# Queries in rows for the last cross attention of a two-layer decoder, and the order of the third part set anew

## The reference

```python
def _L1_xattn_ref(x, context, Wq, Wk, Wv, Wo, bo):   # context: 64 keys of width 96 per sequence
    h, d = (16, 64)
    q = (x @ Wq).reshape(b, n, h, d).transpose(0, 2, 1, 3)
    k = (context @ Wk).reshape(b, -1, h, d).transpose(0, 2, 1, 3)
    v = (context @ Wv).reshape(b, -1, h, d).transpose(0, 2, 1, 3)
    attn = softmax(einsum('bhid,bhjd->bhij', q, k) * d ** -0.5, axis=-1)
    out = einsum('bhij,bhjd->bhid', attn, v)
    return out.transpose(0, 2, 1, 3).reshape(b, n, h * d) @ Wo + bo
x = _layernorm(x + _L1_xattn_ref(x, ctx_768, ...), axis=-1)
```

## Time and profile before

| what | us |
|---|---|
| median of three runs (1770.81 to 1782.97) | 1771.91 |
| the profiled execution's own time | 1776.66 |
| its span, first to last instruction | 1774.6 |
| part one and experts, up to part three's first transposition | about 653 |
| part three, seven full rounds of 133.0 | 931 |
| its last round | 99.2 |

### The profile page before, as it was taken

The page is one execution under the profiler, slowest core; times in us unless marked ns, Lnnn a source line. Parts: engine busy times, 40 slices in busy tenths (PEclk is TensorE's granted clock), DMA queues, the critical chain, the costliest instruction groups (busy, mean ns, idle before and its releaser), DMA issues.

```text
span 1774.6 us, 41025 instructions
## 1 busy us (share of the span) xinstructions
PE 1612.1 (91%) x17280; PEld 1053.8 (59%) x17280; DVE 1086.2 (61%) x2249; ACT 815.9 (46%) x1516; POOL 237.4 (13%) x402
## 2 busy tenths in 40 slices
PE   4899999999978878999999999999999999999985
PEld 1655555555536754675675675675675675675663
DVE  5177777877755454386386387387377277277254
ACT  1456655565542224445345445445445445445423
POOL 1011101110114710011011011011011011011011
PEclk9899999999988879999999999999999999999998
DMA  8331111111118740011011011011011010000000
GB/s 265 151 124 58 53 51 65 53 58 52 54 46 171 117 153 24 20 43 37 16 46 37 7 54 37 2 60 37 1 61 37 2 61 30 8 25 28 5 1 7
DMA packets 64999, 95.68 MB, mean 54 GB/s; under 512 B 9425, under 2 KB 47298, under 8 KB 64083
## 3 DMA queue, kind: packets, MB, share of 16 engines
q1 hardware_dynamic: 61491, 89.20, 15.0%
q0 software_dynamic: 2560, 3.46, 2.2%
q10 hardware_dynamic: 768, 0.40, 0.1%
HBM read 56.03 MB, written 38.80 MB: 53 GB/s over the span
## 4 chain that ended last, share of the span: by engine, by line
PE 72%; DVE 15%; ACT 5%; issue 4%; POOL 2%; DMA 1%; ACTq 0%; DVEq 0%; POOLq 0%; PEldq 0%
PE psum L898 7%; PE psum L804 6%; PE psum L990 6%; PE psum L646 5%; PE psum L885 4%; PE psum L661 3%; PE psum L856 3%; PE psum L671 3%; PE psum L813 3%; ACT prob L1156 3%; DVE kt L1280 3%; DVE va L1280 3%; PE psum L939 2%; PE psum L799 2%; PE psum L703 2%
## 5 line engine op out<-in xcount | busy, mean ns | idle before, releaser
L1156 ACT ACTIVATE prob<-psum 128x1024 f32<-128x1024 f32 (+1 forms) x352 | 322.7, 945 | 329.8 <-PE psum L813 96.0
L1280 DVE TENSOR_REDUCE w_shared<-psum 128x4 bf16<-128x1024 f32 (+1 forms) x160 | 192.8, 1224 | 136.7 <-PE psum L710 94.7
L1458 POOL TENSOR_TENSOR rstd<-moments,eps 128x2 f32<-128x2 f32 x64 | 15.4, 241 | 1005.4 <-DVE moments L1201 1005.4
L1280 DVE TENSOR_REDUCE kt<-psum 128x4 bf16<-128x1024 f32 (+2 forms) x112 | 134.9, 1218 | 15.3 <-PE psum L735 11.5
L804 PE MATMUL psum<-qt,kt 64*128 64x256 f32 x1024 | 131.4, 376 | 0.0
L898 PE MATMUL psum<-prob,v_big 128*64 128x256 f32 x1024 | 124.6, 385 | 0.0
L804 PEld LDWEIGHTS psum<-qt,kt 64*128 64x128 f32 x1024 | 98.6, 189 | 9.9
L939 PE MATMUL psum<-prob,va 128*32 128x256 f32 (+1 forms) x1536 | 95.4, 369 | 1.2 <-ACT prob L1156 1.1
L898 PEld LDWEIGHTS psum<-prob,v_big 128*64 128x64 f32 x1024 | 67.8, 136 | 43.1 <-issue 11.9
L1308 DVE TENSOR_TENSOR qt<-qt,psum 128x1024 f32<-128x1024 f32 x32 | 39.0, 1221 | 85.5 <-PE psum L966 85.0
L1280 DVE TENSOR_REDUCE va<-psum 128x4 bf16<-128x1024 f32 x64 | 76.0, 1215 | 7.3 <-PE psum L747 7.3
(11 more groups left out here) (330 smaller groups left out, 3269.1 us busy)
## 6 DMA issues: line engine op xcount, KB each, us to landing
zd<-kx SPq DMA_DIRECT2D x24, 512.0 KB, 6.0
union<-zd SPq DMA_DIRECT2D x16, 768.0 KB, 4.3
w_late<-ad SPq DMA_DIRECT2D x16, 512.0 KB, 3.7
w_late<-vd SPq DMA_DIRECT2D x16, 512.0 KB, 4.6
ad<-union SPq DMA_DIRECT2D x16, 256.0 KB, 2.1
vd<-union SPq DMA_DIRECT2D x16, 256.0 KB, 2.0
xg<-union SPq DMA_DIRECT2D x16, 192.0 KB, 1.9
w_late<-in_w1T SPq DMA_DIRECT2D x1, 2816.0 KB, 9.8
```

The source lines that it names most:

```text
L1156: nc.scalar.activation(prob_of[a][s][:, slot + 2 * i:slot + 2 * i + 2, 0:n], v.pair(step, i)[:, :, 0:n], ACT.Exp, scale=a.scale).then_inc( ...
L1280: nc.vector.tensor_reduce(dst, src, axis=AX.X, op=ALU.max).then_inc(v.free(step), 1)
```

## The change

L1X alone is computed in another way, and part three's order is new.

- CK, N, P, D and B of L1X are gone, as are the bf16 copies, `ones_x` and `shift_big`.
- S of L1X is one step per half of the queries (128): fp32 matmuls of `xt_x` with all of `a_x`, 16 heads times 64 keys in two banks. DVE takes each row's maximum per head and writes scores minus maximum to SBUF (`by_query`, in `prob`'s slots 4 to 7).
- A new step E per half: ACT takes the exponential in SBUF; DVE sums, takes the reciprocal of 16 columns and multiplies.
- T of L1X is eight transpositions of the weights per half, which ACT copies to `by_key` (`prob`'s slots 0 to 3).
- W of L1X goes by halves of the queries instead of halves of the heads; the matmuls are as many and as large as before.
- D and B remain for L1 only; counters of semaphores follow; three semaphores are merged into others.
- `TURNS3` and `AHEAD3` are new: 144 steps a round instead of 154.

```diff
+def context_scores_steps(s):
+    st = lambda kind, *n: [(kind, L1X, s, i) for i in n]
+    return st("XT", 0) + st("S", 0, 1) + st("E", 0, 1) + st("T", 0, 1) + st("W", 0, 1) + st("L", 0)
...
     main = lambda s: (project_steps(L1, s) + head_steps(L1, s)
-                      + tail_steps(L1, s, [("CK", L1X, s, 0)])
-                      + [("XT", L1X, s, 0)] + project_steps(L1X, s) + head_steps(L1X, s) + tail_steps(L1X, s)
+                      + tail_steps(L1, s) + context_scores_steps(s)
                       + [("XT", L1F, s, 0)] + project_steps(L1F, s) + head_steps(L1F, s) + tail_steps(L1F, s))
...
-AHEAD1, AHEAD3 = (22, 17, 6, 0, 0, 0, 0), (16, 23, 15, 15, 4, 4)
+AHEAD1, AHEAD3 = (22, 17, 6, 0, 0, 0, 0), (16, 22, 15, 15, 4, 4)
... # tensor_step
                 elif a is L1X:
-                    for t in range(2):
-                        last = mm(banks[:, t, :], xb[s][:, 128 * t:128 * t + 128], a_xb[s][:, 512 * which:512 * which + 512],
-                                  start=True, stop=True)
+                    for half in range(2):
+                        last = mm(banks[:, half, :], xt_x[s][:, 128 * which:128 * which + 128],
+                                  a_x[s][:, 512 * half:512 * half + 512], start=True, stop=True)
...
-                    chunks = [(4 * g + 2 * gg + x, banks[:, gg, 256 * x:256 * x + 256], x) for gg in range(2) for x in range(2)]
-                    for c, cols, x in chunks:
-                        both = flat(sel_h[:, 2 * c:2 * c + 2, :])[:, CTX:CTX + 128]
-                        mm(cols, both, shift_big[s], start=(x == 0), stop=False, skip_group_check=True)
-                    for c, cols, x in chunks:
-                        last = mm(cols, a_x[s][:, 128 * c:128 * c + 128], xt_x[s], start=False, stop=True,
-                                  skip_group_check=True)
+                    weights = flat(prob[s][:, 4 + 2 * g:6 + 2 * g, :])
+                    for u in range(8):
+                        last = nc.tensor.transpose(banks[:, u // 4, 128 * (u % 4):128 * (u % 4) + 128],
+                                                   weights[:, 128 * u:128 * u + 128], ident[:, :])
...
+                elif a is L1X:
+                    t = step[3]
+                    for u in range(8):
+                        last = mm(bank[:, t * 128:(t + 1) * 128], by_key[s][t][:, 128 * u:128 * u + 128], vw_x[s][:, u, :],
+                                  start=(u == 0 and t == 0), stop=(u == 7), skip_group_check=True)
... # scalar_step
+            elif kind == "E":
+                act.wait_ge(*v.drained(("S", a, s, step[3])))
+                weights = by_query[s][step[3]]
+                nc.scalar.activation(weights, weights, ACT.Exp, scale=a.scale).then_inc(y.exp_done[s], 1)
+            elif kind == "T" and a is L1X:
+                act.wait_ge(*v.filled(step))
+                copy(by_key[s][step[3]], flat(v.pair(step))).then_inc(v.free(step), 1)
... # vector_step
+            elif kind == "S" and a is L1X:
+                t, scores = step[3], flat(v.pair(step)).rearrange("p (h k) -> p h k", h=16)
+                dve.wait_ge(*v.filled(step))
+                nc.vector.tensor_reduce(largest[s][t], scores, axis=AX.X, op=ALU.max).then_inc(y.r_split[s], 1)
+                dve.wait_ge(y.r_split[s], v.at(9, 4 + t))
+                tt(by_query[s][t], scores, largest[s][t].unsqueeze(2).to_broadcast([128, 16, CTX]), ALU.subtract).then_inc(
+                    v.free(step), 1)
+            elif kind == "E":
+                t = step[3]
+                dve.wait_ge(y.exp_done[s], v.at(2, 1 + t))
+                nc.vector.tensor_reduce(total[s][t], by_query[s][t], axis=AX.X, op=ALU.add).then_inc(y.r_split[s], 1)
+                dve.wait_ge(y.r_split[s], v.at(9, 6 + 2 * t))
+                nc.vector.reciprocal(total[s][t], total[s][t]).then_inc(y.r_split[s], 1)
+                dve.wait_ge(y.r_split[s], v.at(9, 7 + 2 * t))
+                tt(by_query[s][t], by_query[s][t], total[s][t].unsqueeze(2).to_broadcast([128, 16, CTX]), ALU.mult).then_inc(
+                    y.r_parts[s], 1)
```

More of the change, by code:

```diff
@@ L165, in fills @@
     if kind == "P":
-        sums = ["D"] if a.big and step[3] == 0 else []
         if a is L1:
-            return sums + ["O"]
-        if a is L1X:
-            return sums
+            return ["D", "O"] if step[3] == 0 else ["O"]
         return ["O"] if step[3] == 0 else []
@@ L563, in q_cast @@
             def q_cast(self, a, s):
-                cast = lambda x: ("XT" if x is L1X else "C", x, s, 0)
-                return self.count([cast(x) for x in LAYERS[self.tag]], cast(a))
+                return self.count([("C", x, s, 0) for x in LAYERS[self.tag] if x is not L1X], ("C", a, s, 0))
             def k_cast(self, a):
-                return self.at(1, 1) if self.tag == "p1" else self.at(3, CASTS_K[a])
+                return self.at(1, 1) if self.tag == "p1" else self.at(2, CASTS_K[a])
             def narrow(self, a, s):
@@ L761, in tensor_step @@
                                       neg_ident[:, :], start=True, stop=True)
-                elif a is L1X:
-                    for t in range(2):
-                        last = mm(bank[:, t * 128:(t + 1) * 128], peak_w[s][:, t, 0, :], neg_ident[:, :],
-                                  start=True, stop=True)
                 else:
@@ L772, in tensor_step @@
                 g = step[3]
-                if g == 0 and (a is not L1 or step[4] == 0):
+                if a is L1X:
+                    pe.wait_ge(y.r_parts[s], v.wide(1 + g))
+                elif g == 0 and (a is not L1 or step[4] == 0):
                     pe.wait_ge(*v.drained(("N", a, s, 0)))
@@ L869, in tensor_step @@
                 values, turned = ("V", a, s, 3 if a is L1 else 0), step in turned_steps[v.tag]
-                if g == 0 and a is not L1X:
+                if g == 0:
                     pe.wait_ge(*v.drained(values))
@@ L1139, in scalar_step @@
                         last = copy(flat(shift[s][r:r + 4, :, :]), bank[r:r + 4, :])
-                elif a is L1X:
-                    last = copy(shift_big[s][0:16, :], bank[0:16, 0:256])
                 else:
@@ L1163, in scalar_step @@
                     copy(flat(qt[s][:, 2 * g:2 * g + 2, :]), v.bank(*fill)).then_inc(v.free(*fill), 1)
-                elif a is not L1X and g == ROUNDS_T[a] - 1:
+                elif g == ROUNDS_T[a] - 1:
                     fill = ("P", a, s, 0), 0
```

112 lines of the change are left out of this document (39 added, 73 removed).

## The result

The changed kernel takes 1758.8 us (median of 8 runs, 1757.4 to 1762.0), the kernel before 1772.6 (8 runs, 1765.1 to 1783.0). The ratio is 0.9918, with a 95% interval of 0.9898 to 0.9938: about 14 us, or 0.8%, less. That is clear of no change by the interval, but inside the 1% that the prediction named as its line. The forecast was 1756.4. The profiled execution after has a span of 1756.4 us, against 1774.6 before.

A forecast was written before the change was run, and what follows sets the result against it. PE was taken to bound the kernel, busy for 91%, with DVE nearest behind in the first stage. Seven rounds at 1.85 (13.0) plus 2.5 in the last give 15.5 us: 1756.4 from 1771.91; eight-in-ten range 1738 to 1776.

The forecast's parts named there:

- The method's price: L1X in part three: PE gains 2.1 us per sequence, DVE pays 2.2 more, ACT's extra passes stay hidden.
- the DVE chain takes it all: First stage: two-operand and reducing DVE passes cost 0.23 us more, a round gains about 0.5: 1767 us; chance 0.22.
- The walk: Part three's new step list followed with durations: a full round takes 131.15 us, 1.85 less; chance 0.45.
- PE alone counts: Part three: the new order hides the stalls, seven rounds give 4.1 us each, the last 3: 1740; chance 0.24.
- The new stalls: First stage, PE: waits of 0.5, 0.65, 0.45 and 0.55 us and a slower K row, some 2.4 in all.
- a round's length: Full round of part three: 133.0 us before, 131.15 after, with the third stage kept at 38.5.
- The term of the last round: Last round of part three, 99.2 us long: the chain decides, and the last W's statistics come 2.5 us earlier.
- The slack on DVE: First stage, 13.9 to 57.7 us into a round: DVE's work is about 41.5 of 43.8 us, slack 2.3.
- The clock rival: Part three: transpositions read as idle PE, 8 us of each round run at half speed: 1788 us; chance 0.05.

The follow-up runs named there:

- the hidden-stall kernel: Changed kernel with three steps moved earlier in TURNS3 to hide PE's waits for D and for ACT's copy; round 133.6 us, total 1819.9, 1.0017 of before.
- The extra pass: Changed kernel with one more DVE sum over 128x1024 ahead of each E's own sum, four a round; round 136.75 us against 132.43.
- the five repeats: The changed kernel, unchanged, run again on another chip: median of 5 runs 1799.4 us against 1810.8 for the kernel before, ratio 0.9930.
- the half-scores kernel: Changed kernel with half the columns of each L1X score matmul left out; rounds of 131.91 us (first) and 133.05 (others) against 132.43.
- the one with ACT's casts: Changed kernel with L1's casts of K to bf16 moved from DVE to ACT; round 134.45 us, total 1812.8, 1.0018 of before.
- POOL's product: Changed kernel with E's product moved from DVE to POOL; round 133.06 us, 0.6 worse.

## Why the prediction came out

**The method's price was right.** Groups by line and form, VectorE, stage one of the kernel after (busy, mean ns):

```profile
L1254 DVE TENSOR_TENSOR prob<-prob,rsum 128x1024 f32<-128x1024 f32 x4 | 4.9, 1230 | 0.1
L1245 DVE TENSOR_TENSOR prob<-psum,rsum 128x1024 f32<-128x1024 f32 x4 | 4.9, 1224 | 0.1
L1243 DVE TENSOR_REDUCE rsum<-psum 128x16 f32<-128x1024 f32 x4 | 4.9, 1215 | 0.5 <-PE psum L717 0.5
L1250 DVE TENSOR_REDUCE rsum<-prob 128x16 f32<-128x1024 f32 x4 | 4.8, 1199 | 0.0
L1252 DVE RECIPROCAL rsum<-rsum 128x16 f32<-128x16 f32 x4 | 1.0, 253 | 0.1
```

The four passes were put at 1.21 to 1.22 and the reciprocal at 0.25; DVE's round was put at 87 and is 87.7. The rival "the DVE chain takes it all" hung on passes 0.23 us dearer, the first 0.15 of it for the slack; that fell, though DVE turned out to be at its limit all the same (below). PE's round was put at about 125 and is 126.3: it saved 3.5 us of busy time, not 4.1. The scores and the transpositions are nearly as costed (below). The two rounds tell where the 0.6 are: from start to start L1X's old steps take 14.5 us and the new ones 10.7, so 3.8 less; and the projections K and Q of the next pair, which now stand in unbroken rows, take 11.0 instead of 10.0, where the walk had put 0.6 for it.

**The walk was right, nearly step by step.** TensorE's and VectorE's timeline at B0a, and TensorE's at the transpositions, in the kernel after (rows left out between them):

```profile
1146.45 0.71 DVE L1294 SCALAR_TENSOR_TENSOR rdiag<-rpart,part_cols,rsum 64x128 bf16<-64x128 bf16 x2
1147.21 0.61 PE L950 MATMUL psum<-rdiag,spread_b 128*128 128x256 bf16 x4 [0.92 <-DVE rdiag L1294]
1147.66 3.60 PE L717 MATMUL psum<-w_late,qt 128*128 128x512 f32 x8
1151.10 0.38 PE L630 MATMUL psum<-ident,x_in 128*128 128x128 f32 x2
1151.51 0.37 ACT L1062 COPY xt<-psum 128x256 f32<-128x256 f32 x1 [4.69 <-PE psum L630]
1152.03 0.67 PE L661 MATMUL psum<-xt,w_late 128*128 128x256 f32 x2 [0.55 <-ACT xt L1062]
1163.68 1.04 PE L811 MATMUL psum<-ident,prob 128*128 128x128 f32 x8
1164.55 0.38 PE L630 MATMUL psum<-ident,x_tok 128*128 128x128 f32 x2
1181.62 1.13 PE L646 MATMUL psum<-xt_nested,w_qkv 128*128 128x256 f32 x4 [0.19 <-ACT xt_nested L1059]
1191.38 0.29 PE L767 MATMUL psum<-neg_ident,va 128*128 128x128 bf16 x2 [0.23 <-DVE va L1277]
```

B0a waits for D, K0b for ACT's copy, and S is a block of 3.44 us from start to start, two times the 1.72 forecast; eight transpositions take 0.87 to 1.04 start to start, where 0.96 was forecast.

| step | before | walked | after |
|---|---|---|---|
| B0a starts at | 15.5 | 13.5 | 13.8 |
| K0b's wait | | 0.65 | 0.55 |
| Sx0a's wait | | 0.45 | 0.28 |
| Qfb's wait | | 0.55 | 0.19 |
| XTfb | 47.55 | 45.7 | 46.1 |
| Nfb, end of stage one | 60.03 | 57.7 | 58.0 |
| XTfa | 63.7 | 61.6 | 61.7 |
| first T of stage three | 94.5 | 92.65 | 92.8 |
| next round | 134.1 | 131.15 | 132.4 |

Each step up to stage three is within 0.4 us. The new stalls that the walk lists add up to 2.75 us with the slower K row, not to its 2.4; the old round had 1.0 of its own in stage one. The rival "PE alone counts" (a round 4.1 shorter) fell as the prediction argued: the waits at B0a and K0b sit where no neighbour in the list covers them. What the argument lacked is why they are dear to remove, which the hidden-stall kernel showed: DVE has no room to be asked earlier.

**The step that failed: a round's length.** The row for the third stage, 38.50, was taken from a window that ended 1.1 us early; cut at matmuls it is 39.60. The same shift makes a round 134.09 and not 133.0, and, summed over seven rounds, puts the start of the last one at 1675.4 instead of 1681.35. The forecast difference, 1.85 a round, hardly suffered, since the error was taken from both sides; 1.65 was measured, and the 0.2 are missing in stage one (2.04 less instead of 2.3). Seven rounds gave 11.6 instead of 13.0. But the "last round" of 99.2 us was in truth 93.25 plus the end of a full one.

**The term of the last round** (2.5 us less) was mis-sized: it gave nothing in the first pair (93.25 and 93.3). Later it was 96.08 before and 94.45 after, each on a chip of its own, but that is not the change either: N of L1F (b), the last step in which the two kernels differ much, starts at 55.9 before and 55.8 after there (55.96 and 56.03 in the first pair). The rest comes behind it, where the steps are the same and the lower clock lasted longer: 13.7 us from 60.2 on before, 10.2 from 60.6 on after. The walk had looked only at what left the chain. Groups by line, TensorE, last round of the kernel after up to N of L1F (b):

```profile
L811 PE MATMUL psum<-ident,prob 128*128 128x128 f32 x32 | 6.8, 386 | 0.6 <-DVE prob L1254 0.6
L630 PE MATMUL psum<-ident,x_tok 128*128 128x128 f32 x4 | 1.1, 375 | 3.3 <-DVE x_tok L1202 3.3
L630 PE MATMUL psum<-ident,x_norm 128*128 128x128 f32 x2 | 0.7, 449 | 4.6 <-DVE x_norm L1196 4.6
```

The same kinds of rows before:

```profile
L630 PE MATMUL psum<-ident,x_tok 128*128 128x128 f32 x4 | 0.9, 300 | 0.2 <-DVE x_tok L1215 0.2
L630 PE MATMUL psum<-ident,x_norm 128*128 128x128 f32 x2 | 0.4, 301 | 0.0
```

With no steps of a next pair to fill in, PE waits 7.9 us here for normalisations that DVE reaches only behind E's passes, and what comes after such waits runs partly at the lower clock (the transpositions at 386 ns each, against 272 in a full round). The granted clock of the whole last round is 0.91 before and 0.87 after in the first pair, 0.85 and 0.87 later. How much of the missing 2.5 us the chain has and how much the clock was not separated.

**The slack on DVE was overrated.** The prediction counted 41.5 us of work in a stretch of 43.8, 2.3 to spare, and priced the rival with it. The count was right (41.24 in the kernel after); what it was taken to mean was not. The extra pass says otherwise: of 4.8 us added 4.3 arrived. A reading that fits, not tested further: an engine that takes its steps in list order can use idle time only where it falls behind the work that is late. Here 0.5 of the 2.3 could be used.

**What cancelled.** Of the forecast 15.5 us, 11.6 are there by the mechanism named (13.3 in the first pair of profiles, with the two longer rounds of before, which belong to single rounds and not to the method). The last round's 2.5 are not there. The measured 13.8 us between the medians are thus right in the rounds and in part luck beyond them: what the medians hold above 11.6 is no more than the start of the first round varies between kernels with the same first parts. On the chip of the five repeats the medians are 11.4 apart.

**The clock rival.** In the full rounds after, the granted clock is 1.00, transpositions and all, as forecast. The Trainium skill (TensorE: Matmul & The Clock Gate, PE-mode transpose) holds that transposing does not count as being busy in the same way. Blocks of eight transpositions, two within 2.2 us, left the clock where it was, so the trace doesn't show the effect that the rival feared. In other kernels the clock did fall in full rounds, each time behind waits of PE; that is told at the end.

## What to carry to other kernels

When two engines both stand near their limit in a stage, work taken from one and given to the other buys little, and taking work from one alone doesn't show it: relieve one, then the other, then both, and add to each. Before a stall on one engine is hidden by reordering, look at whether the engine that it waits for has idle time ahead of that point; if not, the stall only moves. And cut windows at the same instruction in both kernels, never at round numbers: a microsecond at each boundary is six over seven rounds.

## What the runs showed of the hardware

**The clock falls behind short waits, but not each time.** Windows of 1 us in a full round of the half-scores kernel (length, busy PE, PEld, DVE, ACT, POOL, granted clock):

```profile
1215.77:1216.77 1.00, 0.53 (x8) 0.11 (x4) 0.96 (x2) 0.75 (x2) 0.00 (x0) 1.00 0.00 0
1216.77:1217.77 1.00, 0.00 (x0) 0.00 (x0) 1.00 (x2) 0.18 (x1) 0.00 (x0) 1.00 0.02 8
1217.77:1218.77 1.00, 0.83 (x3) 0.70 (x4) 0.82 (x6) 0.87 (x1) 0.00 (x0) 0.73 0.00 0
1218.77:1219.77 1.00, 1.00 (x4) 0.82 (x3) 1.00 (x2) 0.00 (x0) 0.74 (x4) 0.50 0.72 205
1219.77:1220.77 1.00, 1.00 (x3) 0.80 (x3) 0.93 (x3) 0.84 (x2) 0.82 (x1) 0.50 1.00 348
1220.77:1221.77 1.00, 1.00 (x4) 0.77 (x3) 1.00 (x2) 0.27 (x1) 0.00 (x0) 0.56 0.99 406
```

PE waits 1.64 us (1216.30 to 1217.94) for DVE's addition, works again, and then the granted clock is 0.50, the 1.2 GHz level, for some 3 us. In that kernel's first full round the same wait of 1.64 us was followed by a full clock, and that round was the only one of 131.91; the others took 133.05. The kernel with both stalls hidden had a wait of 1.92 us in every round but the lower clock in three of its seven; those took 135.1 to 135.3, the other four 133.6. The kernel before has one such round too (135.7 in the first profile, 136.0 in the second), and so has the one with ACT's casts (136.0). There no long wait stands ahead of the fall, only three short ones. TensorE's rows and the granted clock behind them, kernel before, first profile:

```profile
1486.25 0.66 PE L949 MATMUL psum<-ident,qt 128*128 128x128 f32 x4 [0.39 <-ACT qt L1167]
1487.37 0.29 PE L768 MATMUL psum<-neg_ident,va 128*128 128x128 bf16 x2 [0.46 <-DVE va L1280]
1487.99 0.44 PE L958 MATMUL psum<-ident,vx 128*128 128x128 f32 x2 [0.34 <-DVE vx L1317]
```

```profile
1488.26:1489.26 1.00, 1.00 (x18) 0.79 (x20) 0.28 (x1) 0.37 (x1) 0.00 (x0) 0.78 0.00 0
1489.26:1490.26 1.00, 1.00 (x14) 0.35 (x6) 0.00 (x0) 0.00 (x0) 0.00 (x0) 0.50 0.00 0
```

And a wait can go by: the kernel with the extra pass has one of 1.55 us at the same place, K of the next pair, in each of its seven rounds, and the granted clock is 1.00 in all of them. So the length of one wait doesn't tell whether the clock falls. That waits are the cause is read from these traces, in which every fall in a full round stands in or behind some; no run took a wait away and nothing else. In the half-scores kernel 3.4 us less work on PE opened the wait of 1.64, and six of its rounds were slower than the changed kernel's. That was in no theory of the first runs.

**POOL's product** takes 1.90 us for 128x1024 in fp32 with a broadcast operand, against 1.23 on DVE. What makes it dear is what it does to DVE's normalisations.

**fp32 on PE**: half of a score's columns, 256, cost half of the time (0.43 of 0.86 us), and eight fp32 transpositions of 128x128 go by in 0.87 us where nothing holds them up.
